# Preparation and attention in one block, with the gate-weight jobs spread over attention steps

## The reference

```python
x = x + tanh(g_xattn[0]) * attention(layernorm(x), ctx, ctx, w_q, w_k, w_v, w_o)   # 16 heads of 64, causal over 64 keys
x = x + tanh(g_ffn[0]) * ffn(layernorm(x), w_gate, w_up, w_down)                   # I = 1536
```

## Time and profile before

| | us |
|---|---|
| median of 3 runs | 1515.35 (1512.8 to 1517.58) |
| profiled execution, device time | 1512.33 |
| its span, first to last instruction | 1510.5 |
| mean granted TensorE clock, share of full speed | 0.947 |
| PE busy | 1331.8 (88%) |
| DVE busy | 1097.1 (73%) |
| ACT busy | 596.8 (40%) |
| POOL busy | 241.3 (16%) |

### The profile page before, as it was taken

The page is one execution under the profiler, slowest core; times in us unless marked ns, Lnnn a source line. Parts: engine busy times, 40 slices in busy tenths (PEclk is TensorE's granted clock), DMA queues, the critical chain, the costliest instruction groups (busy, mean ns, idle before and its releaser), DMA issues. The chain is left out here.

```text
span 1510.5 us, 18719 instructions
## 1 busy us (share of the span) xinstructions
PE 1331.8 (88%) x6141; PEld 1089.7 (72%) x6141; DVE 1097.1 (73%) x1460; ACT 596.8 (40%) x705; POOL 241.3 (16%) x249
## 2 busy tenths in 40 slices
PE   6589999999999985999999989999994009999999
PEld 5468877877886864788888868887883008888887
DVE  5557878878878853667777769998998995455453
ACT  2232232232223212334443335556667973333331
POOL 2112211212212210000100025551101000000000
PEclk9889999999999986999999989999997559999999
DMA  8701211211110117866665689996558863444443
GB/s 290 253 0 36 70 40 53 68 42 49 62 56 35 50 46 300 295 230 236 230 245 191 221 317 309 312 317 214 173 191 322 336 239 120 172 148 167 162 151 118
DMA packets 110998, 259.17 MB, mean 172 GB/s; under 512 B 10848, under 2 KB 23136, under 8 KB 109408
## 3 DMA queue, kind: packets, MB, share of 16 engines
q1 hardware_dynamic: 110656, 258.52, 49.0%
q10 hardware_dynamic: 288, 0.00, 0.0%
HBM read 151.52 MB, written 106.95 MB: 171 GB/s over the span
## 5 line engine op out<-in xcount | busy, mean ns | idle before, releaser
L1065 PE MATMUL gpG<-xph,Wh 128*128 128x512 f32 x384 | 153.1, 399 | 2.0 <-DVE xpl L985 2.0
L1539 PE MATMUL pD<-Wh,xph 128*128 128x512 f32 x384 | 150.3, 391 | 4.6 <-DVE xpl L1518 4.6
L1065 PE MATMUL pU<-xph,Wh 128*128 128x512 f32 x384 | 150.8, 393 | 0.7 <-POOLq L63 0.7
L1065 PE MATMUL gpG<-xph,Wl 128*128 128x512 f32 x384 | 150.7, 393 | 0.0
L1065 PE MATMUL gpG<-xpl,Wh 128*128 128x512 f32 x384 | 150.6, 392 | 0.0
L1065 PE MATMUL pU<-xpl,Wh 128*128 128x512 f32 x384 | 150.5, 392 | 0.0
L1065 PE MATMUL pU<-xph,Wl 128*128 128x512 f32 x384 | 150.3, 392 | 0.0
L1539 PE MATMUL pD<-Wl,xph 128*128 128x512 f32 x384 | 150.1, 391 | 0.0
L1539 PE MATMUL pD<-Wh,xpl 128*128 128x512 f32 x384 | 150.1, 391 | 0.0
L1518 DVE TENSOR_TENSOR xpl<-doq,xph 128x1536 fp32r<-128x1536 int16 (+1 forms) x34 | 56.4, 1664 | 122.8 <-ACT xph L1485 122.8
L968 ACT ACTIVATE gst<-gpG,sc 128x512 f32<-128x512 f32 x96 | 66.4, 692 | 170.3 <-PE gpG L1065 164.5
(11 more groups left out here) (169 smaller groups left out, 2912.6 us busy)
## 6 DMA issues: line engine op xcount, KB each, us to landing
dub<-up_d SPq DMA_DIRECT2D x42, 768.0 KB, 4.7
gate_d<-gst SPq DMA_DIRECT2D x96, 256.0 KB, 2.5
gb<-gate_d SPq DMA_DIRECT2D x32, 768.0 KB, 6.3
up_d<-ust SPq DMA_DIRECT2D x96, 256.0 KB, 4.4
xr<-xn_d SPq DMA_DIRECT2D x9, 1024.0 KB, 6.1
xph<-up_d SPq DMA_DIRECT2D x11, 768.0 KB, 6.0
xpl<-up_d SPq DMA_DIRECT2D x11, 768.0 KB, 6.1
xin<-in_x SPq DMA_DIRECT2D x32, 256.0 KB, 2.7
```

Of the source, the lines that this page charges most:

```text
L1065: mm = pe.matmul(ps[:, :], Ws[:, it, kt * P:(kt + 1) * P], xs[:, kt, :], start=(kt == 0 and Ws is Wh and xs is xh), stop=(kt == KT - 1 and ...
L1539: mm = pe.matmul(pD[4 * t + q][:, :], os_[n][:, cs], Ws[:, it, :], start=(it == 0 and os_ is oh and Ws is Wh), stop=(it == IT - 1 and os_ ...
```

## The change

One function `front_phase` replaces `prepare` and `attend`: one block, no barrier between them.

- **Preparation**: no jobs. SP loads context, w_k, w_q, the first two tiles of x, w_v, x(2), w_o in one transfer, x(3 to 7), and two job pieces. PE does K projection and turning of w_q in four rounds, then four rounds of V; its PSUM tiles are halves of pS. The preparation's buffers share their space with A and V. kbd is set after K, vbd after V. Statistics of tiles 0 and 1 run before the schedule, their normalisation on ACT in V's second round.
- **Jobs**: in the loop of steps (three batches), four a batch, two buffers, and pX as the only bank. Job q: scale and divide in step q+3, integer and turn in step q+4, high, low and store in step q+5; `job_load` of job q+2 in step q+4. PE turns a job at the end of its step, after waiting for xl (pX free). PE's turn of x waits for the job's low part.
- **Normalisations**: both move from DVE to the end of ACT's step, as one activation with scale and bias columns; POOL computes the bias as a third small operation in `rstd`, and does k-3 ahead of k+2. DVE keeps `largest`, now behind xl, and behind six of a chunk step's eight low parts in step 9.
- **Step 8**: PE's turn of x comes after values and chunks, ahead of scores.
- **End**: the reduction over partitions is a PE transposition of the broadcast column and a DVE reduction.

The core of the diff (what only renames or indents is left out; `...` marks it):

```diff
+        JB = 4
+        J = Jobs(mk, ph, "pj", JB, 2, [pX])
+        with ExitStack() as early:
+            wk = sb(early, "wk", [P, KT, INNER], F32)
+            wv = sb(early, "wv", [P, KT, INNER], F32)
+            wq = sb(early, "wq", [P, KT, INNER], F32)
+            cx = sb(early, "cx", [P, 2, H], F32)
+            cT = sb(early, "cT", [P, KT, B * CK], F32)
+        Ah = sb(ph, "Ah", [P, KT, INNER], F32R)
+        Al = sb(ph, "Al", [P, KT, INNER], F32R)
+        Vh = sb(ph, "Vh", [P, PAIRS, H], F32R)
+        Vl = sb(ph, "Vl", [P, PAIRS, H], F32R)
+        pw = [pS[0][:, 0:512], pS[0][:, 512:1024]]
+        pk, pv = pS[1][:, 0:512], pS[1][:, 512:1024]
...
+        def job_at(k, jobs, delay):
+            q = k - 3 - delay
+            return q if jobs and 0 <= q < JB else None
+        def job_src(b, q):
+            q, b = q % JB, b + q // JB
+            return w_src[q][bass.ds(b % 3, 1), :, :].rearrange("a p k -> (a p) k")
+        def job_dst(b, q):
+            return [d[:, bass.ds(q * (3 * 512) + b * 512, 512)] for d in w_dst]
...
+            sp.dma_start(cx[:, :, :], cf.rearrange("(t p) d -> p t d", p=P)).then_inc(ctx_in, 16)
+            load(wk, w_k, wk_in, 0)
+            load(wq, w_q, wq_in, 0)
+            load(wk, w_k, wk_in, 1)
+            load(wq, w_q, wq_in, 1)
+            for j in range(2):
+                load_x(j)
+            for r in range(2):
+                load(wv, w_v, wv_in, r)
+            load_x(2)
+            sp.dma_start(wo[:, :, :], w_o.rearrange("(t p) n -> p t n", p=P)).then_inc(wo_in, 16)
+            for j in range(3, BQ):
+                load_x(j)
+            for q in range(2):
+                job_load(sp, J, 0, q, w_src[q, 0, :, :])
...
+                q = job_at(k, jobs, 2)
+                if q is not None:
+                    job_store(sp, J, b, q, job_dst(b, q))
+                q = job_at(k, jobs, 1)
+                if q is not None:
+                    job_load(sp, J, b, q + J.NJ, job_src(b, q + J.NJ))
...
+                n = j % 2
                 pool.wait_ge(*tile(mean_s, b, j))
                 pool.wait_ge(*tile(used, b, j - 2))
-                pool.tensor_tensor(rs_[:, j % 2, 0:1], mv_[:, j % 2, 1:2], half[:, 1:2], ALU.add).then_inc(eps_s, 1)
-                pool.wait_ge(*tile(eps_s, b, j))
-                pool.tensor_tensor(rs_[:, j % 2, 1:2], rs_[:, j % 2, 0:1], half[:, 0:1], ALU.pow).then_inc(rstd_s, 1)
-            def step(b, k, have):
+                pool.tensor_tensor(rs_[:, n, 0:1], mv_[:, n, 1:2], half[:, 1:2], ALU.add).then_inc(eps_s, 1)
+                pool.wait_ge(*at(eps_s, 2 * BQ * b, 2 * j + 1))
+                pool.tensor_tensor(rs_[:, n, 1:2], rs_[:, n, 0:1], half[:, 0:1], ALU.pow).then_inc(eps_s, 1)
+                pool.wait_ge(*at(eps_s, 2 * BQ * b, 2 * j + 2))
+                pool.sem_inc(apart_p, 1)
+                pool.tensor_scalar(rs_[:, n, 2:3], mv_[:, n, 0:1], rs_[:, n, 1:2], -1.0, ALU.mult, ALU.mult).then_inc(rstd_s, 1)
+            def step(b, k, have, jobs):
+                if have(k - 3):
+                    rstd(b, k - 3, mv2, rs2, mean2_done, eps2_done, rstd2_done, x2_done)
                 if have(k + 2):
                     rstd(b, k + 2, mv, rs, mean_done, eps_done, rstd_done, xn_done)
-                if have(k - 3):
-                    rstd(b, k - 3, mv2, rs2, mean2_done, eps2_done, rstd2_done, x2_done)
...
+                q = job_at(k, jobs, 0)
+                if q is not None:
+                    job_divide(pool, J, b, q)
             schedule(pool, step)
-            pool.wait_ge(sx_red, 1)
-            pool.partition_all_reduce(T1, T0, P, RMAX).then_inc(sx_all, 1)
...
+            def normal(b, j, to, src, mv_, rs_, done):
+                n = j % 2
+                act.activation(to[n][:, :], src[:, :], ACT.Identity, bias=rs_[:, n, 2:3], scale=rs_[:, n, 1:2]).then_inc(done, 1)
...
+                q = job_at(k, jobs, 2)
+                if q is not None:
+                    job_hi(act, J, b, q)
...
+                def normals():
+                    if have(k - 3):
+                        j = k - 3
+                        act.wait_ge(*tile(rstd2_done, b, j))
+                        act.wait_ge(*at(x2_out[j % 2], 8 * BQ * b, 16 * (j // 2)))
+                        act.wait_ge(*tile(x2max_done, b, j - 2))
+                        normal(b, j, x2, x1[j % 2], mv2, rs2, x2_done)
+                    if have(k + 2) and k + 2 >= 2:
+                        j = k + 2
+                        act.wait_ge(*tile(rstd_done, b, j))
+                        act.wait_ge(*tile(xT_ps, b, j - 2))
+                        normal(b, j, xn, xin[j % BQ], mv, rs, xn_done)
...
+                normals()
...
+            for r in range(ROUNDS):
+                copied(kT[:, 2 * r:2 * r + 2, :], (pk, pv)[r % 2], k_ps, r + 1, k_sb)
+                for a in range(2):
+                    copied(wqT[:, 2 * r + a:2 * r + a + 1, :], pw[a], wqT_ps, 2 * r + a + 1, wqT_sb)
+            act.wait_ge(bd_zero, 2)
+            act.wait_ge(k_sb, ROUNDS)
+            diagonal(act, kT, kbd, 0, kbd_set)
+            for r in range(ROUNDS):
+                copied(vT[:, 2 * r:2 * r + 2, :], (pk, pv)[r % 2], v_ps, r + 1, v_sb)
+                if r == 1:
+                    for j in range(2):
+                        act.wait_ge(*tile(rstd_done, 0, j))
+                        normal(0, j, xn, xin[j], mv, rs, xn_done)
+            act.wait_ge(v_sb, ROUNDS)
+            diagonal(act, vT, vbd, 0, vbd_set)
...
+            def largest(b, j):
                 dve.wait_ge(*tile(x2_done, b, j))
-                dve.tensor_reduce(xmx[:, bass.ds(BQ * b + j, 1)], x2[n][:, :], X, ALU.max,
+                dve.tensor_reduce(xmx[:, bass.ds(BQ * b + j, 1)], x2[j % 2][:, :], X, ALU.max,
                                   apply_absolute_value=True).then_inc(x2max_done, 1)
...
+                q = job_at(k, jobs, 2)
+                if q is not None:
+                    job_lo(dve, J, b, q)
                 early = which is not None or not have(BQ)
                 if early and have(k - 3):
@@ -723,20 +672,20 @@
                     scores_down(b, k - 1)
                 if not early and have(k - 3):
                     residual(b, k - 3)
+                q = job_at(k, jobs, 1)
+                if q is not None:
+                    job_integer(dve, J, b, q)
                 if which == 0:
                     some(2)
-                if have(k + 2):
+                if have(k + 2) and k + 2 >= 2:
                     statistics(b, k + 2)
                 some(2 if which == 0 else 1)
+                q = job_at(k, jobs, 0)
+                if q is not None:
+                    job_scale(dve, J, b, q)
                 if have(k - 1):
                     sums(b, k - 1)
-                some(2 if which == 0 else 1)
-                if have(k + 2):
-                    normal(b, k + 2)
-                some(1)
-                if have(k - 3):
-                    normal2(b, k - 3)
-                some(1)
+                some(2 if which == 0 else 3)
...
+                some(2)
+                if have(k - 3):
+                    largest(b, k - 3)
...
+            dve.wait_ge(sx_spread, 1)
+            dve.tensor_reduce(T1, pX[:, 0:P], X, ALU.max).then_inc(sx_scale, 1)
...
-                if which != 0 and have(k) and k >= 0:
-                    scores(b, k)
-                if have(k + 1):
-                    j = k + 1
-                    pe.wait_ge(*tile(xn_done, b, j))
-                    pe.wait_ge(*tile(xl_done, b, j - 1))
-                    for kt in range(KT):
-                        mm = pe.transpose(pX[:, kt * P:(kt + 1) * P], xn[j % 2][:, kt * P:(kt + 1) * P], ident[:, :])
-                    mm.then_inc(xT_ps, 1)
+                def turn_x():
+                    if have(k + 1):
+                        j = k + 1
+                        pe.wait_ge(*tile(xn_done, b, j))
+                        pe.wait_ge(*tile(xl_done, b, j - 1))
+                        q = job_at(k, jobs, 2)
+                        if q is not None:
+                            pe.wait_ge(*at(J.lo_done, JB * b, q + 1))
+                        for kt in range(KT):
+                            mm = pe.transpose(pX[:, kt * P:(kt + 1) * P], xn[j % 2][:, kt * P:(kt + 1) * P], ident[:, :])
+                        mm.then_inc(xT_ps, 1)
+                if which != 0:
+                    if have(k) and k >= 0:
+                        scores(b, k)
+                    turn_x()
                 values(b, k, have)
                 if which == 0:
+                    turn_x()
                     scores(b, k)
+                q = job_at(k, jobs, 1)
+                if q is not None:
+                    pe.wait_ge(*tile(xl_done, b, k + 1))
+                    job_turn(pe, J, b, q, ident)
...
+            def project(w, r, s_in, ready, s_ps):
+                pe.wait_ge(s_in[r // 2], 16)
+                for s, n in ready:
+                    pe.wait_ge(s, n)
```

(19 more changed lines are left out.)

322 lines of the change are left out of this document (100 added, 222 removed).

## The result

| | before | after |
|---|---|---|
| median | 1515.59 us (1512.8 to 1517.58) | 1499.51 us (1497.72 to 1501.14) |
| ratio, with 95% interval | | 0.989 (0.987 to 0.991) |
| profiled execution, span | 1512.33, 1510.5 | 1497.72, 1496.0 |

The account below looks back on a forecast made before the run. Preparation had no single bound; PE bounded ordinary attention steps, a ring 1.1 us behind. -34.6 - 1.6 - 2.9 + 3 x (4.9 + 1.2 + 0.7 + 4.0) = -6.7 took 1512.33 to 1505.6; plus 3.0 for the median, 1508.7 us (1494 to 1527).

Parts of the forecast that it names:

- preparation: Start to first chunk of A: without jobs and with x loaded early, 79.5 becomes 44.9 us, -34.6.
- ring: Steps 3 to 7: transposes, ACT, DVE to sums, POOL's multiplication; job parts ahead of sums lengthen it, +4.9 us a batch.
- The first chunks: First A and V chunks: PE comes in warm and DVE loses a normalisation, -1.6 us in all (-3 to +1).
- step 8: Chunks of A: low part ahead of residual +0.62, unhidden turn of x +0.6; +1.2 us a batch, idle stretch 3.1.
- a fall of the clock: PE slows behind the idle stretches in k = 8 and k = 10, 2.0 us each, +4.0 a batch.
- All stretches from 2.29 us on lost it: Clock rule from the trace: PE kept full speed after idles of 1.87 and 1.91 us, not after 2.29 and 2.70.
- Steps 9 and 10: Chunks of V and after: DVE's largest waits for x2, +1.9 - 1.2 = +0.7 us a batch, plus a clock fall of 2.0.
- The end: End of attention: PE transposition and small DVE operation replace a 4.64 us wait for POOL's reduction, -2.9 us (-4 to 0).
- Removing the normalisations from DVE gives nothing here: Ordinary attention steps: the normalisations stood behind the sums, outside the bounding chain, so no gain was counted.
- The first (the clock stays): Idle stretches of k = 8 and 10: without both falls 1496.7 us, with one 1502.7; chance 0.25.
- The second: Steps with jobs: the ring does not bind, jobs cost PE's four turns, 2.4 us a batch, 1501.2; chance 0.13.
- The third: Steps with jobs: DVE's job parts collide with POOL, 1.3 us x 12 jobs, 1524.5 us; chance 0.26.

Follow-up runs that it names:

- experiment 1: Changed kernel with a job's scale behind sums and xl in VectorE's step: 1492.6 us, ratio 0.984.
- experiment 2: Changed kernel without the gate-weight jobs' computing, pieces only loaded and stored: 1481.7 us, ratio 0.978.
- experiment 7: Changed kernel with unneeded TensorE transpositions: filling idle stretches of steps 8 and 10, 1498.1 us; or sixteen between the last V round and x's first turn, 1501.3 us.
- Experiment 8: Changed kernel with the largest value over partitions found by GpSimd's reduction again at the end of attention: 1504.3 us, ratio 0.992.
- experiment 3: Changed kernel with largest behind all eight low parts of a chunk step instead of six: 1496.5 us, ratio 0.987.
- experiment 5: Changed kernel with both normalisations back on VectorE behind the sums: 1533.4 us, ratio 1.011.
- experiment 9: Changed kernel with VectorE's program unlooped, largest behind all low parts, job's scale behind xl, and x turned ahead of step 8's values: 1480.2 us, ratio 0.977.
- experiment 6: Changed kernel, two edits of step 8: job's low part behind the residual, 1498.3 us; TensorE's turn of x ahead of the values, 1498.5 us.

## Why the prediction was right or wrong

**Right: preparation against ring.** The two large terms were -34.6 and +14.7. The first came as -36.9, the second as +14.7, with each step within 0.2 us of its forecast (12.35, 13.4, 14.0, 14.0, 13.0 against 12.29, 13.2, 13.9, 13.8, 12.8, in the first batch). Its base of 12.39 is the longest of the ordinary steps before; the others take 12.3. Experiments 1 and 2 show that it is the ring for the reason given, parts ahead of the sums. A small part is right by chance: 0.7 us in two of the batches are the jump of VectorE's loop, which was not in the working.

**The preparation, 2.3 us too dear.** The mechanism held, the size was off: the sum added durations (3.62 + 1.04), though ends of matmuls lie over the next starts. From start to start a round is 4.33, and V takes 13.8; the first landing was at 9.58. Some 0.4 of it is chance: the first projection took 4.9 us from start to start in this execution, and 5.0 to 6.5 in the traces of the experiments. The first chunks then gained 0.7 us instead of 1.6, since TensorE waits 1.72 us for VectorE there (46.28).

**Wrong: step 8, 4.9 us too dear, the step of the sum that failed most.** It charged 1.2 and a fall of the clock of 2.0 in each of three batches. The 1.2 came as 1.1. The idle stretch of 2.9 us came too, but in the profiled execution the clock fell behind it once, and a fall cost 1.45 us there (24.27 against 22.82), so 1.45 stand for 6.0. "All stretches from 2.29 us on lost it" was a rule made of two rows, 2.29 and 2.70. In the traces of seven kernels the same stretch brought a fall in 17 of 21 steps, so falls in all batches were the commoner case and the one fall was luck; what they show to be wrong is a fixed term. Fourteen of the 17 falls cost 1.2 to 1.5 us and three 2.7, where 2.0 were charged; three falls would have cost some 4.4 us. The other three executions of the changed kernel took 1.4 to 3.4 us longer than the profiled one, at a mean granted clock of 0.953 against its 0.952; in which steps it fell there isn't on record. The Trainium skill (TensorE: Matmul & The Clock Gate, Part 1) has the fall come from an idle window and not from one gap's length; the traces agree in that a gap of 2.91 us had it in one kernel and not in another.

**Steps 9 and 10: right sum, other terms.** DVE waited for x2 before largest as said (3.23 us idle at 200.76). It came as 0.9 + 1.6 us, where 0.7 + 2.0 were charged; the 1.6 is the difference to the 12.5 of a step 10 whose clock stayed. What such a fall costs the kernel is less, which the prediction did not see: where the clock stayed in step 10 and the jump follows, step 3 took 13.7 to 14.4 us instead of 13.0 (experiments 1, 7 and 8), so 0.7 to 1.4 of the 1.6 come back. Experiment 3 shows how much of step 9 is this one instruction's place, 3.6 us a batch.

**The end, 0.9 us too dear.** It was to gain 2.9 and gained 3.8, and the last batch another 0.4. The wait and the operation were put at 1.3; they were 0.57 and 0.29. Experiment 8 prices GpSimd's reduction at 3.6 us.

**The normalisations: a sentence that was true and misleading.** "Removing the normalisations from DVE gives nothing here" holds for the steps before. In the changed kernel it is a condition for the whole gain: with both back on VectorE it would have been 1533, slower than before (experiment 5). The sum was not hurt by it, but it calls without gain the edit on which the rest stands. What was overlooked is that the job's turn, put behind xl in TensorE's order and ahead of the transposes, makes VectorE's tail part of the ring.

**The rivals.** The first (the clock stays) happened in part, in two of six places, the largest part of the miss. The second is refuted by the 0.72 us of idle time ahead of the transposes and by experiment 1. The third did not occur: beside POOL's small operations the dequantisation took 0.69, not 1.41. (By the prediction's own numbers the kernel would have been slower than before from some 0.55 us a job on, 6.65 us over 12 jobs; its 0.9 holds only for slower by more than 4.5 us.) But the contention of which the Trainium skill (GPSIMD Engine Reference, 8. Key points) speaks is in the trace from the other side: POOL's pow took 1.01 while VectorE dequantised and 0.55 otherwise (122.24 and 124.17), off every path; and VectorE's L207 took 0.85 instead of 0.18 beside POOL's long multiplication, in experiments 1 and 9.

**Median and profile.** The forecast added 3.0 us from profiled run to median, as before had it; after has 1.8. That is another 1.2 of the 9.2 us by which the time was missed.

## What to carry to other kernels

When work is moved into a loop that has one bound, cost it by its place: the same 1.1 us was free behind the sums and cost 1 us ahead of them, and an innocent wait on another engine (the turn's, for xl) can pull the free part into the ring as well. Sum starts to starts, not durations. Where a gain at the end of a loop's body doesn't arrive, look at the first instruction behind the jump: there an engine may start late whatever its data do.

## What the hardware showed that was not expected

**VectorE can need more than 5 us from one side of a loop's jump to the other.** In the changed kernel and seven of its variants with a loop and jobs (experiments 1, 3, 6, 7 and 8) 5.1 to 6.0 us lie between its last instruction of step 10 and the first of step 3. As 3.95 us or so of this are a wait for data without the loop too, step 3 loses less: 0.7 us in the changed kernel, up to 2.7 where the data come earlier (14.99 in experiment 3). For 205 to 225 us the changed kernel and that of experiment 3 have four packets on the instruction queue; written out there are none, and step 3 is 12.29. That instructions are fetched again at the jump fits this. The length of the loop's body does not explain it: the kernel of experiment 5 has two more VectorE instructions a step, no packets at its jump, and went on after 0.39 us, as the kernel before did after 0.80 (245.61). What decides whether the fetch is needed, for instance where the body lies in the program, was not tried.

**The clock's fall doesn't follow from the idle time alone.** In step 8, behind the stretch that ends with the residual or the job's low part, it fell in 17 of 21 steps after 2.9 us idle, in 4 of 15 after 2.03 to 2.31 us, and in none of three after 1.87 us (the kernel before). In the middle group are none of three after 2.30 (experiment 6), but one of three after 2.31 (experiment 2). So falls are more frequent behind the longer stretch, but no length from 2.03 us on settles it. A fall cost 1.2 to 2.7 us of its step.
